# Key and value projections: values ahead of keys in three edge chunks, and all row terms added in one stretch

## The chip, the cores and the metric

The program runs on one core of a Trainium2 chip. The metric is the device time of one execution in microseconds (us), the median of several runs. Engines: PE (TensorE, matmuls), DVE (VectorE), ACT (ScalarE), POOL (GpSimd), SP (SyncE, which here only issues DMAs).

## The reference, cut to what matters

Two batches of 512 tokens with 1024 channels and a context of 1024 positions per batch go through four blocks. The change touches the first three, at their start:

```
x = x + tanh(g)*matmul(fake_quant(layernorm(x)), fake_quant(ctx))   # block 1
x = x + tanh(g)*(x1 @ W_org.T + sum_e coeff_e*(x1 @ down_e) @ up_e) # block 2, x1 = layernorm(x)
k = ctx @ Wk;  v = ctx @ Wv                                         # for block 3, attention
x = x + tanh(g)*(softmax(q k^T/sqrt(32)) v) @ Wo                    # block 3, q = layernorm(x) @ Wq
x = x + tanh(g)*moe(layernorm(x))                                   # block 4, two of three experts
```

With fake_quant(a) = (q - z)*s, the product in block 1 is a matmul of shifted integers plus a term for each row of x (`rterm`, from the row sums of the quantised x) and a term for each column of the context (`CB`, from its column sums).

## The kernel before, in words

Float32 matmuls are made of three bf16 ones: each operand is split into a high part and a low part (hi, lo), and hi*hi, hi*lo, lo*hi are summed in PSUM. Every engine has its own instruction list, written out by hand, and semaphores tie them together.

**Keys and values.** The context comes in 32 chunks of 128x1024 float32, in the order of the table `CHUNKS`: kind T (the transposed context, for keys and values) and kind N (the natural one, quantised for block 1). Chunks 0 to 7 are T of batch 0. Chunks 8 to 11 are T of batch 1, and its other four stand at 14, 16, 18 and 21 among N chunks. All from 22 on are N. SP loads them through a ring of 6 buffers, and waits in `load_context` until DVE is done with chunk n - 6 (`c_done`). For a T chunk, ACT writes the high part (L1076) and DVE the low part (L1345). For an N chunk, ACT scales (L1078), and DVE clips and rounds (L1390, L1392).

PE runs `kv_tile` (before, L643) once per T chunk. 12 matmuls of 512 columns (L666) add to the keys in banks 0 to 3, then 24 matmuls of 256 columns (L672) add to the values in banks 4 to 7. After the eighth chunk of a batch the banks are emptied in `kv_out`. ACT copies keys high (L1101) and half of the values (L1104), DVE copies the other half of the values (L1404) and takes keys low (L1409). Both wait for `kv_step`, that is for the whole of the eighth chunk. PE then begins the first chunk of batch 1 with keys, and waits for `k_lo` (DVE is done with the two banks).

**Block 1.** After the last T chunk PE sums columns (`column_sums`, L696, bank 4 + 2b and the next, so V must be out of them). It runs `quantised_tile(t)` for the 8 token tiles (L720, 16 matmuls each), whose operand SP turns by DMA (`turn_x`, L405) once all keys and values are through. The tiles write banks 0 to 3, so the keys must be out of them (`k_lo` 8). DVE makes the column term (`column_terms`, L1485). ACT adds the row term to each x tile (`add_rows`, L1108). POOL adds the column term behind it (`add_columns`, L548). DVE then adds the matmul result (`quantised_update`, L1502) and takes the layer norm of block 2 of it (L1358 and the small operations after it). ACT scales the tile (`scale_rows`, L1189), PE turns it (`turn_behind`, L708), ACT takes the high part (`turned_out`, L1195) and DVE the low part (`lo_parts`, L1492, in the middle of the next but one update).

ACT's list before, in the part the change touches:

```
chunks(26, 30); kv_out(1); chunks(30, 32)
for t in range(TB): add_rows(t)        # t = 0..3
scale_rows(0); scale_rows(1)
for t in range(2, TT):
    turned_out(t - 2); scale_rows(t)
    if t < 4: add_rows(2 * t); add_rows(2 * t + 1)
```

**Block 2.** PE goes through the LoRA queries (`lora_query`), eight hidden tiles (`lora_hidden`) and eight token tiles (`token_tile`), all L641. POOL splits the weights in two parts each (L516, L518), in the order down, lora_q, up, org, q, o, between its other work. Before the first token tile PE waits for all eight `org` weights (`wt_done`).

Of the kernel before, what the change touches and what calls it, by code (L numbers as in the profile page):

```python
# [32 lines left out]
KVD = KV_HEADS * HD  # L33
# [11 lines left out]
WT_AT = {name: sum(n for _, n in WT_LAYOUT[:i]) for i, (name, _) in enumerate(WT_LAYOUT)}  # L45
# [71 lines left out]
def build(nc, x, ctx_nat, ctx_t, wts, lora_q, lora_keys, scalars, gate_w, w1, b1, w2, b2, out):  # L117
    with ExitStack() as ctx:
# [3 lines left out]
        def sem(name):  # L122
            return ctx.enter_context(nc.semaphore(name))
# [6 lines left out]
        V = sb("V", [P, B * KT * KVD], F32)  # L130
# [57 lines left out]
        kb = [[R[1][:, b * half_r + i * 2 * SC:b * half_r + (i + 1) * 2 * SC] for i in range(2)] for b in range(B)]  # L188
# [27 lines left out]
        bank = [ctx.enter_context(nc.psum_tensor(f"bank{i}", [P, HALF], F32)) for i in range(8)]  # L216
# [16 lines left out]
        wt_done = sem("wt_done")  # L233
# [12 lines left out]
        xq_done = sem("xq_done")  # L246
        xq_t = [sem(f"xq_t{t}") for t in range(TT)]
        kv_step = sem("kv_step")
        rowq_done = sem("rowq_done")
        ln_bias = sem("ln_bias")  # L250
        k_hi = sem("k_hi")
        k_lo = sem("k_lo")
        v_act = sem("v_act")
# [380 lines left out]
        def _(pe):  # L634
# [8 lines left out]
                return mm  # L643


            def kv_tile(k, first, again, begin=False):
                def c(t, n0, n):
                    return t[:, k * D + n0:k * D + n0 + n]

                def w(t, n0, n):  # L650
                    return t[:, k * HALF + n0:k * HALF + n0 + n]

                for m in range(2):
                    if again:
                        pe.wait_ge(k_lo, 2 * (m + 1))
                    for a, r in ((kv_h, ct_h), (kv_h, ct_l), (kv_l, ct_h)):
                        if begin and m == 0:
                            if a is kv_l:
                                pe.wait_ge(kv_first, 2)
                            elif r is ct_l:  # L660
                                pe.wait_ge(c_done, 1)
                            else:
                                pe.wait_ge(kv_first, 1)
                                pe.wait_ge(c_act, 1)
                        for h in range(2):
                            mm = pe.matmul(bank[2 * m + h][:, :], w(a, m * P, P), c(r, h * HALF, HALF),  # L666
                                           start=first and a is kv_h and r is ct_h, stop=False, skip_group_check=True)
                for t in range(KT):
                    if again and t % 2 == 0:
                        pe.wait_ge((v_act, v_dve)[t // 4], t // 2 % 2 + 1)  # L670
                    for a, r in ((ct_h, kv_h), (ct_h, kv_l), (ct_l, kv_h)):
                        mm = pe.matmul(bank[4 + t // 2][:, (t % 2) * KVD:(t % 2 + 1) * KVD], c(a, t * P, P),  # L672
                                       w(r, KVD, KVD), start=first and t % 2 == 0 and a is ct_h and r is kv_h,
                                       stop=False, skip_group_check=True)
                return mm

            def keys_values(b):
                for k in range(KT):
                    begin = b == 0 and k == 0
                    if not begin:  # L680
                        if b == 0:
                            pe.wait_ge(wt_done, k // 2 + 1)
                        pe.wait_ge(c_done, CHUNKS.index(("T", b, k)) + 1)
                    mm = kv_tile(k, k == 0, b > 0 and k == 0, begin)
                    mm.then_inc(kv_step, 1)

            for _ in range(WARM):
                pe.matmul(bank[7][:, 0:P], identb[:, :], identb[:, :], start=True, stop=True)
# [112 lines left out]
            def token_tile(m, t, par, w_h, w_l, lora):  # L801

                pe.wait_ge(x_up, 2 * (m - 1))
                outs = [bank[2 * par][:, :], bank[2 * par + 1][:, :]]
                for k in range(KT):
                    cols = bass.ds(k * D + t * P, P)
                    mm = triple(outs, XTh[:, cols], XTl[:, cols],
                                [w_h[:, k * D + h * HALF:k * D + (h + 1) * HALF] for h in range(2)],
                                [w_l[:, k * D + h * HALF:k * D + (h + 1) * HALF] for h in range(2)],
                                k == 0, k == KT - 1 and not lora)  # L810
                if lora:
                    if isinstance(t, int) and t == 0:
                        pe.wait_ge(h_lo, B * JT)
                    for j in range(JT):
                        cols = bass.ds(j * D + t * P, P)
                        mm = triple(outs, HT_h[:, cols], HT_l[:, cols],
                                    [up_h[:, j * D + h * HALF:j * D + (h + 1) * HALF] for h in range(2)],
                                    [up_l[:, j * D + h * HALF:j * D + (h + 1) * HALF] for h in range(2)],
                                    False, j == JT - 1)
                mm.then_inc(nat_mm, 1)  # L820
# [28 lines left out]

            pe.wait_ge(cv_done, 4)  # L850
            pe.wait_ge(h_lo, JT + 1)
            pe.wait_ge(wt_done, WT_AT["q"])
            for t in range(TT):
                token_tile(TT + t, t, t % 2, org_h, org_l, True)
            first_queries()
# [207 lines left out]
        def _(act):  # L1063
# [30 lines left out]
                    act.wait_ge(rowq_done, t)  # L1094
                act.activation(junk_q, XQ[:, t * D:(t + 1) * D], ACT.Copy, accum_out=rowq[:, t:t + 1]).then_inc(rowq_done, 1)

            def kv_out(b):
                act.wait_ge(kv_step, KT * (b + 1))
                for i in (0, 1, 2, 3, 4, 5) if b == 0 else (4, 5, 0, 1, 2, 3):
                    if i < 4:  # L1100
                        act.activation(kb[b][0][:, i * HALF:(i + 1) * HALF], bank[i][:, :], ACT.Copy).then_inc(k_hi, 1)  # L1101
                    else:
                        at_v = b * KT * KVD + (i - 4) * HALF
                        act.activation(V[:, at_v:at_v + HALF], bank[i][:, :], ACT.Copy).then_inc(v_act, 1)  # L1104

            def add_rows(t):
                act.wait_ge(rterm_done, 1)
                act.activation(X[:, t * D:(t + 1) * D], X[:, t * D:(t + 1) * D], ACT.Identity,  # L1108
                               bias=rterm[:, t:t + 1]).then_inc(x_row, 1)

            def chunks(first, last):
                for n in range(first, last):
                    chunk(n)
# [20 lines left out]
            root(4, 0)  # L1134
            chunks(8, 9)
            scale_x(4)
            chunks(9, 11)
            kv_out(0)
            chunks(11, 12)
            row_sum(3)  # L1140
            root(5, 1)
            chunks(12, 15)
# [11 lines left out]
            chunks(23, 26)  # L1154
            row_sum(7)
            act.wait_ge(rowq_done, TT)
            chunks(26, 30)
            kv_out(1)
            chunks(30, 32)
            for t in range(TB):  # L1160
                add_rows(t)
            act.wait_ge(const_in, 48)

# [49 lines left out]
            for t in range(2, TT):  # L1213
                turned_out(t - 2)
                scale_rows(t)
                if t < 4:
                    add_rows(2 * t)
                    add_rows(2 * t + 1)
            lora_exp(0)
            turned_out(TT - 2)  # L1220
            hidden_out(0)
# [87 lines left out]
            for s in range(SLOTS):  # L1309
                b = s // TOPK  # L1310
# [24 lines left out]
        def _(dve):  # L1335
# [62 lines left out]
                dve.wait_ge(xq_sc, t + 1)  # L1398
                clip_round(xn[t % 2][:, :], XQ[:, t * D:(t + 1) * D], xq_clip, t, xq_done)

            def kv_out(b):
                def values(i):
                    at_v = b * KT * KVD + (2 + i) * HALF
                    dve.tensor_copy(V[:, at_v:at_v + HALF], bank[6 + i][:, :]).then_inc(v_dve, 1)  # L1404

                def keys_lo(i):
                    dve.wait_ge(k_hi, 4 * b + i + 1)
                    cols = slice(i * HALF, (i + 1) * HALF)
                    dve.tensor_tensor(kb[b][1][:, cols], bank[i][:, :], kb[b][0][:, cols], ALU.subtract).then_inc(k_lo, 1)  # L1409

                dve.wait_ge(kv_step, KT * (b + 1))
                values(0)
                if b == 0:
                    for i in range(4):
                        keys_lo(i)
                    values(1)
                else:
                    values(1)
                    for i in range(4):
                        keys_lo(i)  # L1420


            def constants():
                dve.wait_ge(sc_in, 16)
# [27 lines left out]
            def chunks(first, last):  # L1452
                for n in range(first, last):
                    chunk(n)
# [9 lines left out]
            x_step(3)  # L1464
            chunks(7, 8)
            x_step(4)
            chunks(8, 11)
            kv_out(0)
            x_step(5)
            chunks(11, 16)  # L1470
            x_step(6)
# [1 line left out]
            x_step(7)  # L1473
            chunks(20, 23)
            quantise_x(7)
            chunks(23, 29)
            kv_out(1)
            dve.wait_ge(rowq_done, TT)
            dve.tensor_scalar(rterm[:, :], rowq[:, :], qc[:, 5:6], qc[:, 4:5], ALU.add, ALU.mult).then_inc(rterm_done, 1)
            chunks(29, 32)  # L1480

            def column_terms(b):
                dve.wait_ge(cs_mm, b + 1)
# [392 lines left out]
```

## Time and profile before

| | us |
|---|---|
| median of 3 runs | 1254.35 (1251.49 to 1257.41) |
| the profiled execution | 1259.31 |
| its span in the profile | 1257.5 |
| PE busy in the span | 1222.9 (97%) |
| DVE busy | 821.9 (65%) |
| ACT busy | 476.4 (38%) |
| POOL busy | 681.7 (54%) |

The span is the time from the first to the last instruction, and the profiled execution lasts 1.8 us longer. Times in the rows are us from the span's start. A share of busy time is a mean over stages. The change lies between 44 and 205 us, so it is the rows of that part that tell.

### The profile page before, as it was taken

To read this page: it belongs to the slowest core of one execution; us is meant where nothing else is said; L and a number is where in the kernel's file an instruction comes from. 1 tells how busy PE (TensorE), PEld (TensorE's weight loads), DVE (VectorE), ACT (ScalarE), POOL (GpSimd) and SP (SyncE) were. 2 spreads that over 40 slices of the span, in tenths; PEclk is the share of its full clock that TensorE was granted. 3 is DMA by queue.
4 is the path that set the end of the run, shared out by engine and by line. 5 is a ranking of instruction groups with operands and counts; after the bars stand their busy time and mean duration, and the time that the engine had idled before them with its cause. 6 is when DMAs were issued, how large, how long until landed. Compare 5 with 4: busy or idle time off the path is not lost.

```text
span 1257.5 us, 16924 instructions
## 1 busy us (share of the span) xinstructions
PE 1222.9 (97%) x6504; PEld 512.1 (41%) x6504; DVE 821.9 (65%) x1417; ACT 476.4 (38%) x826; POOL 681.7 (54%) x300
## 2 busy tenths in 40 slices
PE   8998899999999899999999999999989999999998
PEld 6564444444444322222222222234434444444444
DVE  7997731433456778998999989335538855737622
ACT  4774521000100467777777677743242010010000
POOL 6005898500033478888989889870164553624510
PEclk9999999999999999999999999999989999999999
DMA  9566143311332145453545444443493443523301
GB/s 356 171 245 154 65 134 115 86 34 34 79 129 92 59 96 113 107 117 87 120 106 112 95 103 104 84 84 60 113 213 105 140 126 100 184 85 101 117 15 52
DMA packets 86764, 141.20 MB, mean 112 GB/s; under 512 B 49056, under 2 KB 59296, under 8 KB 82592
## 3 DMA queue, kind: packets, MB, share of 16 engines
q1 hardware_dynamic: 45840, 94.03, 23.7%
q0 software_dynamic: 4608, 33.56, 13.2%
q10 hardware_dynamic: 36240, 12.60, 5.2%
q8 instruction: 48, 0.79, 0.3%
q14 instruction: 28, 0.23, 0.1%
HBM read 85.49 MB, written 10.49 MB: 76 GB/s over the span
## 4 chain that ended last, share of the span: by engine, by line
PE 79%; DVE 12%; DMA 2%; POOL 2%; ACT 2%; issue 1%; ACTq 0%; SPq 0%; POOLq 0%; DVEq 0%
PE bank L641 46%; PE bank L879 9%; DVE mxp L1616 8%; PE bank L866 6%; PE bank L948 5%; PE bank L911 5%; PE bank L666 3%; PE bank L672 3%; DVE xn L1606 2%; DMA stage_c<-w_in 1%; DMA R<-R 1%; POOL R L607 1%; POOL R L629 1%; PE bank L720 1%; POOL X L548 1%
## 5 line engine op out<-in xcount | busy, mean ns | idle before, releaser
L1616 DVE TENSOR_REDUCE mxp<-bank 128x1 f32<-128x512 f32 x512 | 320.6, 680 | 60.6 <-PE bank L866 60.3
L1261 ACT ACTIVATE R<-bank 128x512 f32<-128x512 f32 x512 | 273.9, 602 | 116.7 <-PE bank L948 113.5
L641 PE MATMUL bank<-XTh,R 128*128 128x512 bf16 x896 | 279.3, 381 | 4.7 <-POOL R L629 4.5
L607 POOL TENSOR_TENSOR R<-R 128x2048 f32<-128x2048 f32 x48 | 218.6, 4555 | 35.4 <-ACT R L1261 29.4
L641 PE MATMUL bank<-R 128*128 128x512 bf16 x960 | 209.2, 379 | 0.0
L641 PE MATMUL bank<-XTl,R 128*128 128x512 bf16 x448 | 170.7, 381 | 0.0
L629 POOL TENSOR_TENSOR R<-stage_pair,R 128x1024 bf16<-128x1024 f32 x32 | 75.4, 2371 | 138.6 <-DVE R L1770 84.1
L641 PEld LDWEIGHTS bank<-R 128*128 128x128 bf16 x960 | 93.9, 98 | 113.3
L866 PE MATMUL bank<-R 96*128 96x512 bf16 x352 | 134.6, 382 | 4.6 <-DVE mxp L1616 3.0
L879 PE MATMUL bank<-R,stage_c 128*32 128x512 f32 x1024 | 137.1, 607 | 0.5 <-ACT R L1261 0.5
L948 PE MATMUL bank<-R 98*128 98x512 bf16 x352 | 134.4, 382 | 2.1 <-ACT R L1261 2.1
L641 PEld LDWEIGHTS bank<-XTh,R 128*128 128x128 bf16 x896 | 88.0, 98 | 112.1 <-POOL R L629 5.4
L516 POOL TENSOR_TENSOR R<-stage_pair,zero 128x1024 f32 (+1 forms) x35 | 67.2, 1920 | 77.4 <-DMA stage_pair<-wts_in 74.5
L629 POOL TENSOR_TENSOR R<-stage_c,R 128x1024 bf16<-128x1024 f32 x32 | 73.7, 2315 | 59.8 <-DVE R L1770 50.2
L1319 ACT ACTIVATE R<-bank,b1t 128x512 f32<-128x512 f32 x32 | 21.6, 686 | 198.1 <-PE bank L641 198.1
L866 PEld LDWEIGHTS bank<-R 96*128 96x128 bf16 x352 | 34.2, 97 | 112.2 <-DVE mxp L1616 84.7
L518 POOL TENSOR_TENSOR R<-stage_pair,R 128x1024 f32 (+1 forms) x35 | 75.9, 2167 | 5.3 <-POOL R L516 4.7
L1606 DVE RECIPROCAL xn<-p_total 128x128 f32<-128x128 f32 x64 | 59.2, 937 | 27.6 <-POOL xn L589 27.6
L607 POOL TENSOR_TENSOR stage_pair<-R 128x2048 f32<-128x2048 f32 x16 | 73.7, 4604 | 4.3 <-ACT R L1261 3.2
L911 PE MATMUL bank<-R,XTh 128*128 128x512 bf16 x256 | 69.7, 379 | 0.8 <-issue 0.8
L1815 DVE SCALAR_TENSOR_TENSOR X<-xn,TV,X 128x512 f32<-128x512 f32 x32 | 67.4, 2147 | 0.1
L1084 ACT ACTIVATE lnv<-lnv 128x1 f32<-128x1 f32 x32 | 6.5, 202 | 158.7 <-DVE lnv L1365 138.3
(194 smaller groups left out, 1502.0 us busy)
## 6 DMA issues: line engine op xcount, KB each, us to landing
stage_pair<-wts_in SPq DMA_DIRECT2D x35, 512.0 KB, 3.7
R<-R POOLq DMA_DIRECT2D x16, 1024.0 KB, 6.9
stage_pair<-R POOLq DMA_DIRECT2D x16, 1024.0 KB, 7.0
stage_pair<-w_in SPq DMA_DIRECT2D x32, 512.0 KB, 3.5
stage_c<-w_in SPq DMA_DIRECT2D x32, 512.0 KB, 3.6
R<-q_scr SPq DMA_DIRECT2D x48, 128.0 KB, 2.4
XTh<-ctx_t_in SPq DMA_DIRECT2D x11, 512.0 KB, 7.7
XTh<-ctx_nat_in SPq DMA_DIRECT2D x9, 512.0 KB, 3.9
```

What stands on the lines that cost most here:

```text
L518: pool.tensor_tensor(lo, stage_w[stage][:, :], hi, ALU.subtract).then_inc(wt_done, 1)
L607: pool.tensor_tensor(PS[(0, 1, 2, 1)[j]], PB[2 * j % 4], PB[2 * j % 4 + 1], ALU.add).then_inc(p_add, 1)
L629: pool.tensor_tensor(lo[:, cols], stage_e[(n - N_WT) % RING_E][:, :], hi[:, cols], ALU.subtract).then_inc(wt_done, 1)
L641: mm = pe.matmul(o, a, m, start=first and a is ah and bs is bh, stop=last and a is al)
L866: pe.matmul(bank[s_bank(u)][:, :], QS[g % 3][0:96, h * S + qt * P:h * S + (qt + 1) * P], KS[g % 3][0:96, kh * HALF:(kh + 1) * HALF], start ...
L879: mm = pe.matmul(out_bank[h * HD:(h + 1) * HD, :], weights, probs[:, h * S:(h + 1) * S], start=first, stop=last)
L911: mm = pe.matmul(outs[h], a[i][:, cols], b[i][:, k * D + h * HALF:k * D + (h + 1) * HALF], start=k == 0 and i == 0, stop=k == KT - 1 and i ...
L948: pe.matmul(bank[t_bank(g, t)][:, :], KS[g % 3][0:98, kt * P:(kt + 1) * P], QS[g % 3][0:98, h * S:(h + 1) * S], start=True, stop=True).the ...
L1261: act.activation(PB[kt % 4][:, h * S:(h + 1) * S], bank[t_bank(g, t)][:, :], ACT.Exp, scale=float(HD) ** -0.5).then_inc(exp_done, 1)
L1606: dve.reciprocal(rec[:, cols], p_sum[:, cols]).then_inc(rec_done, 1)
L1616: dve.tensor_reduce(mxp[head // REP % 2][:, m, n // 2, n % 2:n % 2 + 1], bank[s_bank(u)][:, :], AX.X, ALU.max).then_inc(s_max, 1)
L1815: dve.scalar_tensor_tensor(out=xh, in0=b2b[:, hc], scalar=TV[:, j * TT + t:j * TT + t + 1], in1=xh, op0=ALU.mult, op1=ALU.add).then_inc(eo ...
```

## The change

1. `kv_tile` is split into `keys_tile` and `values_tile`. In three edge chunks (the eighth of batch 0, the first and the eighth of batch 1) the values come ahead of the keys. The value tiles are taken in the order 0, 1, 4, 5, 2, 3, 6, 7.
2. A new semaphore `kv_vals` rises after the values of the eighth chunk. `kv_out` is split into `values_out`, which waits for `kv_vals`, and `keys_out`, which waits for `kv_step`, on ACT and on DVE.
3. The chunks of context are placed anew around them. Batch 0: ACT and DVE have only chunk 8 ahead of `values_out(0)`, chunk 9 between the two, chunk 10 behind. Batch 1: chunks up to 30 come ahead of `values_out(1)`, chunk 31 between, and none behind. The row term `rterm` is made ahead of `values_out(1)`.
4. ACT adds all eight row terms in one stretch behind `keys_out(1)`.
5. Token tile 0 of block 2 waits for each `org` weight apart, in place of all eight.

```diff
+            def keys_tile(b, k):
                 for m in range(2):
-                    if again:
+                    if b > 0 and k == 0:
                         pe.wait_ge(k_lo, 2 * (m + 1))
...
+            def values_tile(b, k):
+                for t in (0, 1, 4, 5, 2, 3, 6, 7):
+                    if b > 0 and k == 0 and t % 2 == 0:
                         pe.wait_ge((v_act, v_dve)[t // 4], t // 2 % 2 + 1)
...
-                    mm = kv_tile(k, k == 0, b > 0 and k == 0, begin)
-                    mm.then_inc(kv_step, 1)
+                    if k == KT - 1:
+                        values_tile(b, k).then_inc(kv_vals, 1)
+                        keys_tile(b, k).then_inc(kv_step, 1)
+                    elif b > 0 and k == 0:
+                        values_tile(b, k)
+                        keys_tile(b, k).then_inc(kv_step, 1)
+                    else:
+                        keys_tile(b, k)
+                        values_tile(b, k).then_inc(kv_step, 1)
...
                 for k in range(KT):
+                    if lora and t == 0:
+                        pe.wait_ge(wt_done, WT_AT["org"] + k + 1)
...
-            pe.wait_ge(wt_done, WT_AT["q"])
...
-            def kv_out(b):
+            def values_out(b):
+                act.wait_ge(kv_vals, b + 1)
...
+            def keys_out(b):
                 act.wait_ge(kv_step, KT * (b + 1))
...
-            chunks(9, 11)
-            kv_out(0)
-            chunks(11, 12)
+            values_out(0)
+            chunks(9, 10)
+            keys_out(0)
+            chunks(10, 12)
...
-            chunks(26, 30)
-            kv_out(1)
-            chunks(30, 32)
-            for t in range(TB):
+            chunks(26, 31)
+            values_out(1)
+            chunks(31, 32)
+            keys_out(1)
+            for t in range(TT):
                 add_rows(t)
...
                 scale_rows(t)
-                if t < 4:
-                    add_rows(2 * t)
-                    add_rows(2 * t + 1)
...
-            chunks(8, 11)
-            kv_out(0)
+            chunks(8, 9)
+            values_out(0)
+            chunks(9, 10)
+            keys_out(0)
+            chunks(10, 11)
...
-            chunks(23, 29)
-            kv_out(1)
+            chunks(23, 31)
             dve.wait_ge(rowq_done, TT)
             dve.tensor_scalar(rterm[:, :], rowq[:, :], qc[:, 5:6], qc[:, 4:5], ALU.add, ALU.mult).then_inc(rterm_done, 1)
-            chunks(29, 32)
+            values_out(1)
+            chunks(31, 32)
+            keys_out(1)
```

What this moves, on the two engines that PE waits for. First DVE's list at the end of keys and values, before (V from a bank is a values copy, R from a bank a keys low, rterm the row term, XTh or stage_c a chunk in its ring buffer, and the last row the column term):

```order
L1404 COPY V<-bank 128x512 x2
L1409 TENSOR_TENSOR R<-bank,R 128x512 x4
L1479 TENSOR_SCALAR rterm<-rowq,qc 128x8
L1390 TENSOR_SCALAR XTh<-XTh 128x1024
L1392 TENSOR_SCALAR R<-XTh 128x1024
L1390 TENSOR_SCALAR stage_c<-stage_c 128x1024
L1392 TENSOR_SCALAR R<-stage_c 128x1024
L1390 TENSOR_SCALAR stage_c<-stage_c 128x1024
L1392 TENSOR_SCALAR R<-stage_c 128x1024
L1485 TENSOR_SCALAR R<-bank,qc 128x512 x2
```

and in the changed kernel (where the lines have other numbers):

```order
L1404 TENSOR_SCALAR XTh<-XTh 128x1024
L1406 TENSOR_SCALAR R<-XTh 128x1024
L1404 TENSOR_SCALAR stage_c<-stage_c 128x1024
L1406 TENSOR_SCALAR R<-stage_c 128x1024
L1486 TENSOR_SCALAR rterm<-rowq,qc 128x8
L1419 COPY V<-bank 128x512 x2
L1404 TENSOR_SCALAR stage_c<-stage_c 128x1024
L1406 TENSOR_SCALAR R<-stage_c 128x1024
L1426 TENSOR_TENSOR R<-bank,R 128x512 x4
L1494 TENSOR_SCALAR R<-bank,qc 128x512 x2
```

Two of the three last chunks moved ahead of the values copies, the third stands between values and keys, and nothing is left between the keys and the column term.

ACT's list in block 1, before (V and R from a bank are the copies, X the row terms, lnv the root of a norm, xn the scaled rows, XTh from a bank the high parts of a turned tile):

```order
L1104 ACTIVATE V<-bank 128x512 x2
L1101 ACTIVATE R<-bank 128x512 x4
L1078 ACTIVATE stage_c<-stage_c,sc,rs 128x1024 x2
L1108 ACTIVATE X<-X,rterm 128x1024 x4
L1084 ACTIVATE lnv<-lnv 128x1
L1189 ACTIVATE xn<-X,lnv 128x1024
L1084 ACTIVATE lnv<-lnv 128x1
L1189 ACTIVATE xn<-X,lnv 128x1024
L1195 ACTIVATE XTh<-bank 128x4x128 x2
L1084 ACTIVATE lnv<-lnv 128x1
L1189 ACTIVATE xn<-X,lnv 128x1024
L1108 ACTIVATE X<-X,rterm 128x1024 x2
```

and in the changed kernel:

```order
L1114 ACTIVATE V<-bank 128x512 x2
L1091 ACTIVATE stage_c<-stage_c,sc,rs 128x1024
L1119 ACTIVATE R<-bank 128x512 x4
L1123 ACTIVATE X<-X,rterm 128x1024 x8
L1097 ACTIVATE lnv<-lnv 128x1
L1206 ACTIVATE xn<-X,lnv 128x1024
L1097 ACTIVATE lnv<-lnv 128x1
L1206 ACTIVATE xn<-X,lnv 128x1024
L1212 ACTIVATE XTh<-bank 128x4x128 x2
L1097 ACTIVATE lnv<-lnv 128x1
L1206 ACTIVATE xn<-X,lnv 128x1024
L1212 ACTIVATE XTh<-bank 128x4x128 x2
```

The two pairs of row terms that stood between the scaled rows and the high parts of tiles 1 and 2 are gone from there.

## Rows read from the trace of the kernel before

**Rows 1.** The page: the chain that ended last, by engine.

```profile
PE 79%; DVE 12%; DMA 2%; POOL 2%; ACT 2%; issue 1%; ACTq 0%; SPq 0%; POOLq 0%; DVEq 0%
```

**Rows 2.** The chain in order of time: start, us, what.

```profile
91.85 2.59 PE bank L666 x12
...
194.14 156.80 PE bank L641 x726
```

**Rows 3.** Timeline of PE, 51 to 146: start, us, engine, line, work [idle before <-releaser].

```profile
53.54 4.44 PE L666 MATMUL bank<-R 128*128 128x512 bf16 x12 [2.10 <-DVE R L1409]
...
98.49 3.61 PE L696 MATMUL bank<-R,onesb 128*128 128x512 bf16 x16 [1.43 <-DVE V L1404]
...
130.69 1.06 PE L708 MATMUL bank<-identf,xn 128*128 128x128 f32 x8 [3.10 <-DVE XTl L1492]
...
138.31 1.23 PE L708 MATMUL bank<-identf,xn 128*128 128x128 f32 x8 [3.10 <-DVE XTl L1492]
139.32 5.18 PE L720 MATMUL bank<-R 128*128 128x512 bf16 x16
...
145.22 0.38 PE L641 MATMUL bank<-XTh,stage_c 128*128 128x512 bf16 x1
```

**Rows 4.** Windows: us, busy PE, PEld, DVE, ACT, POOL, granted PE clock, DMA share, GB/s.

```profile
54.00:56.00 2.00, 2.00 (x6) 0.71 (x5) 2.00 (x5) 2.00 (x4) 0.00 (x0) 0.50 0.23 89
56.00:93.00 37.00, 37.00 (x254) 24.70 (x253) 35.75 (x70) 28.83 (x34) 0.00 (x0) 0.98 0.72 249
132.00:134.00 2.00, 2.00 (x11) 0.91 (x10) 1.86 (x7) 0.96 (x1) 0.50 (x1) 1.00 0.00 0
140.00:142.00 2.00, 2.00 (x6) 0.72 (x5) 1.89 (x6) 1.34 (x2) 1.92 (x3) 0.50 0.00 0
```

**Rows 5.** Timeline of DVE, 49 to 147.

```profile
49.03 2.36 DVE L1345 TENSOR_TENSOR R<-XTh,R 128x1024 bf16<-128x1024 f32 x2 [1.12 <-ACT R L1076]
...
52.10 2.48 DVE L1409 TENSOR_TENSOR R<-bank,R 128x512 bf16<-128x512 f32 x4
...
97.10 1.29 DVE L1404 COPY V<-bank 128x512 f32<-128x512 f32 x2 [3.70 <-PE bank L672]
...
101.30 0.69 DVE L1390 TENSOR_SCALAR XTh<-XTh 128x1024 f32<-128x1024 f32 x1
...
105.29 1.40 DVE L1485 TENSOR_SCALAR R<-bank,qc 128x512 f32<-128x512 f32 x2
109.20 1.41 DVE L1502 SCALAR_TENSOR_TENSOR X<-bank,qc,X 128x512 f32<-128x512 f32 x2 [2.51 <-POOL X L548]
...
125.30 1.40 DVE L1502 SCALAR_TENSOR_TENSOR X<-bank,qc,X 128x512 f32<-128x512 f32 x2
...
129.25 1.29 DVE L1492 TENSOR_TENSOR XTl<-bank,XTh 128x512 bf16<-128x512 f32 x2 [1.82 <-ACT XTh L1195]
...
140.54 1.40 DVE L1502 SCALAR_TENSOR_TENSOR X<-bank,qc,X 128x512 f32<-128x512 f32 x2
...
146.24 1.40 DVE L1502 SCALAR_TENSOR_TENSOR X<-bank,qc,X 128x512 f32<-128x512 f32 x2
```

**Rows 6.** Timeline of ACT, the row terms.

```profile
102.24 4.29 ACT L1108 ACTIVATE X<-X,rterm 128x1024 f32<-128x1024 f32 x4
...
126.57 2.17 ACT L1108 ACTIVATE X<-X,rterm 128x1024 f32<-128x1024 f32 x2
```

**Rows 7.** Timeline of POOL, 106 to 205.

```profile
106.83 9.28 POOL L548 TENSOR_TENSOR X<-X,R 128x1024 f32<-128x1024 f32 x4 [78.45 <-DVE R L1485]
...
127.84 4.66 POOL L548 TENSOR_TENSOR X<-X,R 128x1024 f32<-128x1024 f32 x2 [3.62 <-ACT X L1108]
...
140.00 1.90 POOL L558 TENSOR_TENSOR stage_c<-stage_c,zero 128x1024 bf16<-128x1024 f32 x1
...
204.96 1.89 POOL L516 TENSOR_TENSOR R<-stage_pair,zero 128x1024 f32 x1 [2.79 <-PE bank L641]
```

**Rows 8.** Timeline of SP's queue: the turning of the quantised x.

```profile
97.09 11.01 SPq L405 DMA_TRANSPOSE R<-XTl x8
```

More of the change, by code:

```diff
@@ L248, in build @@
         kv_step = sem("kv_step")
+        kv_vals = sem("kv_vals")
         rowq_done = sem("rowq_done")
@@ L643, in triple, with chunk_part, weight_part @@
                 return mm
[L646 to L651, printed above, removed]
+            def chunk_part(t, k, n0, n):
+                return t[:, k * D + n0:k * D + n0 + n]
+            def weight_part(t, k, n0, n):
+                return t[:, k * HALF + n0:k * HALF + n0 + n]
+            def keys_tile(b, k):
                 for m in range(2):
-                    if again:
+                    if b > 0 and k == 0:
                         pe.wait_ge(k_lo, 2 * (m + 1))
                     for a, r in ((kv_h, ct_h), (kv_h, ct_l), (kv_l, ct_h)):
-                        if begin and m == 0:
+                        if b == 0 and k == 0 and m == 0:
                             if a is kv_l:
@@ L665, in kv_tile @@
                         for h in range(2):
[L666 to L669, printed above, removed]
+                            mm = pe.matmul(bank[2 * m + h][:, :], weight_part(a, k, m * P, P), chunk_part(r, k, h * HALF, HALF),
+                                           start=k == 0 and a is kv_h and r is ct_h, stop=False, skip_group_check=True)
+                return mm
+            def values_tile(b, k):
+                for t in (0, 1, 4, 5, 2, 3, 6, 7):
+                    if b > 0 and k == 0 and t % 2 == 0:
                         pe.wait_ge((v_act, v_dve)[t // 4], t // 2 % 2 + 1)
                     for a, r in ((ct_h, kv_h), (ct_h, kv_l), (ct_l, kv_h)):
-                        mm = pe.matmul(bank[4 + t // 2][:, (t % 2) * KVD:(t % 2 + 1) * KVD], c(a, t * P, P),
-                                       w(r, KVD, KVD), start=first and t % 2 == 0 and a is ct_h and r is kv_h,
+                        mm = pe.matmul(bank[4 + t // 2][:, (t % 2) * KVD:(t % 2 + 1) * KVD], chunk_part(a, k, t * P, P),
+                                       weight_part(r, k, KVD, KVD), start=k == 0 and t % 2 == 0 and a is ct_h and r is kv_h,
                                        stop=False, skip_group_check=True)
@@ L678, in keys_values @@
                 for k in range(KT):
-                    begin = b == 0 and k == 0
-                    if not begin:
+                    if b > 0 or k > 0:
                         if b == 0:
@@ L1095, in row_sum @@
                 act.activation(junk_q, XQ[:, t * D:(t + 1) * D], ACT.Copy, accum_out=rowq[:, t:t + 1]).then_inc(rowq_done, 1)
-            def kv_out(b):
-                act.wait_ge(kv_step, KT * (b + 1))
[L1099 to L1104, printed above, removed]
+            def values_out(b):
+                act.wait_ge(kv_vals, b + 1)
+                for i in range(2):
+                    at_v = b * KT * KVD + i * HALF
+                    act.activation(V[:, at_v:at_v + HALF], bank[4 + i][:, :], ACT.Copy).then_inc(v_act, 1)
+            def keys_out(b):
+                act.wait_ge(kv_step, KT * (b + 1))
+                for i in range(4):
+                    act.activation(kb[b][0][:, i * HALF:(i + 1) * HALF], bank[i][:, :], ACT.Copy).then_inc(k_hi, 1)
             def add_rows(t):
@@ L1399, in quantise_x, with values_out, keys_out @@
                 clip_round(xn[t % 2][:, :], XQ[:, t * D:(t + 1) * D], xq_clip, t, xq_done)
-            def kv_out(b):
-                def values(i):
+            def values_out(b):
+                dve.wait_ge(kv_vals, b + 1)
+                for i in range(2):
                     at_v = b * KT * KVD + (2 + i) * HALF
                     dve.tensor_copy(V[:, at_v:at_v + HALF], bank[6 + i][:, :]).then_inc(v_dve, 1)
-                def keys_lo(i):
+            def keys_out(b):
+                dve.wait_ge(kv_step, KT * (b + 1))
+                for i in range(4):
                     dve.wait_ge(k_hi, 4 * b + i + 1)
@@ L1409, in keys_lo @@
                     dve.tensor_tensor(kb[b][1][:, cols], bank[i][:, :], kb[b][0][:, cols], ALU.subtract).then_inc(k_lo, 1)
[L1411 to L1420, printed above, removed]
             def constants():
```

## The prediction

> **What bounds the kernel now.** I read the chain of waits first. PE holds 79% of it and DVE 12% [rows 1], so only a place where PE waits, or where PE's waits are set by another engine, can give time. Then I read PE's timeline over the part that the change touches, to find these places. There are three.
>
> At the boundary of the batches PE stands still for 2.10 us until DVE has taken keys low. The 12 matmuls behind it take 4.44 us [rows 3], where the same 12 take 2.59 elsewhere, 0.216 each [rows 2]. The granted clock is 0.50 there, the lower of PE's two levels (1.2 GHz in place of 2.4), in the window 54 to 56 [rows 4]. Together 2.10 + 1.85 = 3.95 us.
>
> At the end of keys and values PE waits 1.43 us for DVE's copies of V [rows 3].
>
> In block 1, PE waits for the low part of each turned tile, up to 3.10 us a time [rows 3]. What sets the pace is the chain of updates on DVE. Three updates start at 125.30, 140.54 (two later) and 146.24 [rows 5]. The two periods up to 140.54 are 7.62 us each, the one behind it is 5.70. The long ones hold a 1.82 us wait for ACT, which had put a pair of row terms (2.17 us) ahead of the high part [rows 5, 6]. From 145.22 on PE has its own work as its bound: one piece of the chain, from 194.14, is 156.8 us of matmuls without a break [rows 2]. So a start of that stretch that is earlier by n us makes everything behind it earlier by n.
>
> DVE is the second bound. From 56 to 93 it is busy 35.75 of 37 us [rows 4]. It then idles 3.70 us ahead of its V copies, since PE is not done [rows 5].
>
> **The change, part by part.**
>
> *Boundary of the batches.* Values of the eighth chunk come first, so both engines empty banks 4 to 7 while PE makes keys (2.59 us). The next chunk begins with values (2.62 us), and in that time the keys leave banks 0 to 3. DVE took its first two keys-low operations until about 2 us after PE's end, and all four until 3.15 us (52.10 + 2.48 against 53.54 - 2.10) [rows 5]; the keys banks are wanted 2.62 and 3.9 us after it. PE's wait and the slow stretch behind it go: PE ended keys and values at 97.06 (98.49 - 1.43), and would end them at 93.1. What is late next is DVE. It does the same work in another order, but must wait for ACT between: before, the last keys-low is followed by one V copy (0.6 us), now by the low part of chunk 10 (1.18, half of 2.36) [rows 5]. So `x_step(5)` starts some 0.6 later, and as DVE has no slack until 93, it ends chunk 28 at 93.40 (97.10 - 3.70) + 0.6 = 94.0. This first gain is therefore worth nothing yet: PE stands before DVE.
>
> *End of keys and values.* DVE now has two more chunks ahead of its V copies. One chunk costs 1.33 us ((105.29 - 101.30)/3 [rows 5]). 94.0 + 2.66 + 0.2 for the row term = 96.85, V copies 1.25, done at 98.1. PE's column sums start at 98.2, against 98.49. PE idles 5.1 us there, not 1.43. Then come chunk 31 (to 99.4), keys low 2.4 (to 101.8) and the column term at 101.85, which started at 105.29 before [rows 5]: 3.45 us earlier. It also needs the column sums, 3.45 us of PE (16 x 0.216): 98.2 + 3.45 = 101.65. Tile 0 needs the keys out, 101.8, as before. ACT has the copies and the scaling of chunk 31 beside it, and its eight row terms (4.29/4 = 1.07 each [rows 6]) run from about 98 to 106.5, each ahead of its column term. The first root that ACT owes DVE comes after that.
>
> *PE's clock.* The idle 5.1 us is the new cost. The rows have four gaps on PE, of 2.10, 1.43, 3.10 and 3.10 us. After the first and the last the clock fell (0.50), after the others it did not (1.00 at 132 to 134, behind the first 3.10; 16 matmuls in 3.61 us behind the 1.43) [rows 3, 4]. A fall cost 1.85 us over 12 matmuls, and 1.57 over the 16 matmuls at 139.32 (5.18 against 3.61) [rows 3]. Bounds: 0 (no fall), and 16 + 16 matmuls of column sums and tile 0 all at the lower level, 32 x 0.216 = 6.9. I take 1.7, the mean of the two rows, since the gap is longer than any of the four. The column sums then end at 103.35, the column term starts at 103.4, and 3.45 shrinks to 1.9 us. POOL's first addition follows it (1.54 us behind its start, 106.83), and the first update starts 2.37 us later still [rows 5, 7]: 107.3 against 109.20. Tile 0 ends at 106.8, in time. The Trainium skill, page "TensorE: Matmul & The Clock Gate", section "HAM oscillation — how this bites in real kernels", tells that PE idle between bursts of matmuls can put its clock back to the half rate, so that each next burst begins slow. By that rule alone the fall at 98 is certain; by the count of rows it is two of four.
>
> *Row terms in one stretch.* With none between scaled rows and high part, the two periods of 7.62 become 5.70 like the next one: 2 x 1.92 = 3.84 us. They are not on ACT's path any more, where before they were late for POOL as well (3.62 us idle on POOL) [rows 7]. PE must keep up: its work from tile 0 to `turn_behind(2)` puts the turned tiles at most 1 us behind DVE's chain, with gaps of about 1.4 in place of 3.10. So the second fall of the clock goes too. It was worth 0.4 us: 145.22 lay 4.68 behind the update at 140.54, and would lie 4.3 behind it (2.05 to the low part, 1.27 for it, 0.1, and 0.88 for eight transposes).
>
> *The weights behind it.* POOL works from 140.00 to 202.17 (204.96 - 2.79), 62.2 us, all of it weight splits, and PE needs its last `org` part at about 204.7 [rows 7]. If POOL stayed and PE moved, this would bind. But POOL's first four additions start 1.9 earlier, and the other four find their rows ready: 104.9 + 9.3, + 8.1 for two weight splits (116.11 to 124.22), + 9.3 = 131.6 in place of 140.00. That is 8.4 earlier, more than PE moves. `lora_q` takes two more operations, some 4 us, and PE wants it at 139. The waits per weight at token tile 0 have nothing to hide: cost 0, and if POOL were late they would soften it.
>
> *Queues.* SP issues the eight turning DMAs (11.01 us from 97.09 [rows 8]) once PE is through, so 4 us earlier. Tile 0 is not waiting for the first, as it starts no earlier. SP's keys out and weights behind them come as early. The ring loads of chunks 29 to 31 follow DVE, 0.6 later, and have the time of the chunks before to land.
>
> **Sum**, against the profiled execution: 1.9 + 3.84 + 0.4 = 6.15 us, so 1259.31 - 6.15 = 1253.2. That execution is 5 us above the median. One difference can be in this very place: the 1.85 us after the boundary gap need not be there in each execution, as gaps without a fall show. Where they are missing, the kernel before is faster by 1.85 (PE ends sooner, DVE has 3.70 to spare) and the changed one is not. The gain is then 4.3. I take the middle, 5.25, off the median of the runs: **1249.1 us**.
>
> **The rivals.**
>
> *A, the forecast:* DVE bounds the end of keys and values, one fall of the clock behind the long gap. 4.3 to 6.15 us, 1248.2 to 1250.05. Chance 0.47.
>
> *B, the clock holds or costs little:* the column term really is 3.45 earlier. 3.45 + 3.84 + 0.4 = 7.7, less up to 1.85 as above: 1246.7 to 1248.5. For it: a gap of 3.10 without a fall. Against it: the gap is 5.1. Chance 0.20.
>
> *C, the gain of the row terms is swallowed:* PE or POOL becomes the bound of block 1, for instance because `lora_q` or the turned tiles are late, and only the first term is left: 1.9 us, 1252.5; with neither, 1254.35. For it: PE is slack by some 1 us only. Against it: POOL's 8.4 us. Chance 0.22.
>
> *D, slower:* the clock, once down at 98, stays at the lower level through column sums and tiles 0 to 3, 96 matmuls x 0.216 = 20.7 us, as the tiles are then PE's bound. Less the 7.7: +13, 1267. It is slower from 7.7 us of such loss on (36 matmuls). For it: there are small gaps between these tiles that could hold it down. Against it: both falls in the rows were over within 12 to 16 matmuls. Chance 0.04.
>
> The remaining 0.07 is for what I do not see, either side.
>
> **How the numbers follow.** A measurement of this kernel can tell about 0.5%, 6.3 us, from no change; faster by that is below 1248.1. Of A a quarter lies there with the scatter of the runs (5.9 us between highest and lowest of three), 0.12; of B four fifths, 0.16; of C none; the remainder 0.04, and the scatter of the median itself lifts the total to 0.38. Slower: D and a share of the remainder, 0.05. Within: 0.57. The range goes from B with scatter below, 1244.5, to C without either term, 1253.
>
> **What would show it.** PE has no wait at the boundary, and its clock stays at 1.00 there. PE ends keys and values near 93.1 and the column sums start near 98.2, with 0.50 granted behind them. DVE has no idle time ahead of its V copies. The column term starts near 103.4. All updates from the second on are 5.7 us apart, and the first LoRA query is at about 139. Wrong would be: a gap at 93 much shorter than 5 us; the gap between updates above 6; a wait of PE for POOL in block 2.

## The result, and the profile after

| | before | changed |
|---|---|---|
| median of 20 runs, us | 1256.83 (1251.49 to 1263.28) | 1253.85 (1249.73 to 1256.35) |
| ratio of the times | | 0.9972, 95% interval 0.9963 to 0.9981 |
| the profiled execution, us | 1259.31 | 1254.74 |
| its span, us | 1257.5 | 1252.9 |
| first LoRA query on PE, us from the start | 145.22 | 139.30 |

The change makes the kernel faster by 0.28%, which is 3.5 us (2.4 to 4.7 by the interval, so clear of zero). The forecast was 1249.1 us in a range from 1244.5 to 1253, and the measured median lies above it.

In the profiled pair nearly each step came where the prediction had put it. PE's timeline of the changed kernel, the part that answers to [rows 3]:

```profile
53.64 5.34 PE L668 MATMUL bank<-R 128*128 128x512 bf16 x24
...
90.11 2.75 PE L668 MATMUL bank<-R 128*128 128x512 bf16 x12
97.90 5.50 PE L708 MATMUL bank<-R,onesb 128*128 128x512 bf16 x16 [5.03 <-DVE V L1419]
103.24 7.07 PE L732 MATMUL bank<-R 128*128 128x512 bf16 x32
...
132.70 1.06 PE L720 MATMUL bank<-identf,xn 128*128 128x128 f32 x8 [1.18 <-DVE XTl L1501]
133.60 3.62 PE L732 MATMUL bank<-R 128*128 128x512 bf16 x16
138.40 1.06 PE L720 MATMUL bank<-identf,xn 128*128 128x128 f32 x8 [1.18 <-DVE XTl L1501]
139.30 0.38 PE L642 MATMUL bank<-XTh,stage_c 128*128 128x512 bf16 x1
```

The boundary of the batches has no wait any more: keys of two chunks follow each other, 24 matmuls in 5.34 us. PE ends keys and values at 92.87, and idles 5.03 us. The column sums behind that gap take 5.50 us, against 3.61 before. The gaps in block 1 are 1.18 us in place of 3.10.

The windows of the changed kernel (columns as in [rows 4]) give the clock:

```profile
54.00:56.00 2.00, 2.00 (x11) 0.88 (x9) 2.00 (x4) 2.00 (x4) 0.00 (x0) 1.00 0.78 306
56.00:92.80 36.80, 36.80 (x254) 24.60 (x252) 35.59 (x70) 28.55 (x34) 0.00 (x0) 1.00 0.73 240
93.00:97.90 4.90, 0.00 (x1) 0.03 (x2) 4.80 (x10) 4.82 (x8) 0.00 (x0) 0.70 1.03 209
98.00:100.00 2.00, 2.00 (x6) 0.61 (x6) 1.97 (x4) 2.00 (x3) 0.00 (x0) 0.50 0.97 187
102.00:104.00 2.00, 2.00 (x11) 0.92 (x10) 0.49 (x1) 2.00 (x3) 0.00 (x0) 1.00 0.95 183
```

At the boundary it stays at 1.00. It falls in the idle time (0.70 is the mean of it), is at 0.50 when the column sums begin, and is back at 1.00 from 102 on.

DVE's timeline of the changed kernel, which answers to [rows 5]:

```profile
96.52 1.28 DVE L1419 COPY V<-bank 128x512 f32<-128x512 f32 x2
97.71 0.68 DVE L1404 TENSOR_SCALAR stage_c<-stage_c 128x1024 f32<-128x1024 f32 x1
98.43 0.69 DVE L1406 TENSOR_SCALAR R<-stage_c 128x1024 bf16<-128x1024 f32 x1
99.04 2.48 DVE L1426 TENSOR_TENSOR R<-bank,R 128x512 bf16<-128x512 f32 x4
103.51 1.41 DVE L1494 TENSOR_SCALAR R<-bank,qc 128x512 f32<-128x512 f32 x2 [1.99 <-PE bank L708]
107.45 1.41 DVE L1511 SCALAR_TENSOR_TENSOR X<-bank,qc,X 128x512 f32<-128x512 f32 x2 [2.53 <-POOL X L549]
...
123.54 1.40 DVE L1511 SCALAR_TENSOR_TENSOR X<-bank,qc,X 128x512 f32<-128x512 f32 x2
...
134.94 1.40 DVE L1511 SCALAR_TENSOR_TENSOR X<-bank,qc,X 128x512 f32<-128x512 f32 x2
```

DVE has no idle time ahead of its V copies, since it now comes to them after PE is through. The column term starts at 103.51 (forecast 103.4) and had to wait 1.99 us for the slow column sums. The first update starts at 107.45 (forecast 107.3, before 109.20). Two periods lead from 123.54 to 134.94, 5.70 each.

POOL (answers to [rows 7]) has its four last additions in one piece, and its wait for PE ahead of the `q` weights is longer, so no weight holds PE:

```profile
122.45 9.29 POOL L549 TENSOR_TENSOR X<-X,R 128x1024 f32<-128x1024 f32 x4
131.70 1.89 POOL L559 TENSOR_TENSOR stage_c<-stage_c,zero 128x1024 bf16<-128x1024 f32 x1
...
199.05 1.89 POOL L517 TENSOR_TENSOR R<-stage_pair,zero 128x1024 f32 x1 [5.35 <-PE bank L642]
```

So the profiled pair has 5.92 us at the LoRA query and still 5.91 at 199 us (204.96 - 199.05), where 6.15 was forecast. At the end of the span 4.6 us are left (1257.5 - 1252.9). Yet the runs gave 3.5. Two questions remained: which part of the change gives the time, and why the runs show less than the profiles.

### The profile page after: what moved, and what is told of

It reads as the page before. It is cut to its first block, busy times and chain, and to the rows that moved or that the text cites. A ratio compares the mean times of both kernels' runs of the same rounds, so it can differ in the third digit from the quotient of the medians.

```text
span 1252.9 us, 16926 instructions
## 1 busy us (share of the span) xinstructions
PE 1223.0 (98%) x6504; PEld 511.6 (41%) x6504; DVE 822.5 (66%) x1417; ACT 476.8 (38%) x826; POOL 681.5 (54%) x300
## 4 chain that ended last, share of the span: by engine, by line
PE 76%; DVE 16%; DMA 2%; issue 2%; POOL 2%; ACT 1%; ACTq 0%; SPq 0%; POOLq 0%; DVEq 0%
PE bank L642 46%; PE bank L892 9%; DVE mxp L1625 8%; PE bank L879 6%; PE bank L961 5%; PE bank L924 5%; DVE xn L1615 2%; PE bank L678 2%; PE bank L668 1%; DVE R L1406 1%; DMA stage_c<-w_in 1%; DVE R L1359 1%; DMA R<-R 1%; POOL R L608 1%; POOL R L630 1%
## 5 line engine op out<-in xcount | busy, mean ns | idle before, releaser
L1805 DVE CAST R<-R 128x512 bf16<-128x512 f32 x32 | 17.5, 547 | 75.1 <-ACT R L1333 75.1
```

## The experiments

All were timed beside the kernel before, in two batches on one chip each. The medians of before were 1256.94 us (29 runs) and 1257.13 us (23 runs). The gains below are the ratio's. The plain differences of the medians are up to 1.1 us away from them (6.1 in place of 7.2 for the widest), and lie within the intervals. The rival theories: the two terms of the sum are both real; or only one of them is, and the other comes from a slow stretch in the profiled execution of before that other executions don't have.

### The row terms alone

```diff
-            for t in range(TB):
+            for t in range(TT):
                 add_rows(t)
...
                 scale_rows(t)
-                if t < 4:
-                    add_rows(2 * t)
-                    add_rows(2 * t + 1)
```

> The kernel before, with nothing but the eight row terms in one stretch behind the last chunks. Theory (both terms of the sum are real and add up): update periods on DVE fall from 7.62 to 5.70 us twice, the first update stays at about 109.2 (107.3 if the clock did not fall at the batch boundary), the first LoRA query comes at about 141; 3.8 to 4.3 us faster than before in the mean. Rival (the row terms have slack elsewhere and the gain of the change is only in DVE's order): no more than 1 us.

Measured: 1253.32 us, ratio 0.9974 (0.9961 to 0.9987), which is 3.3 us. DVE's timeline of this kernel:

```profile
109.23 1.41 DVE L1499 SCALAR_TENSOR_TENSOR X<-bank,qc,X 128x512 f32<-128x512 f32 x2 [2.54 <-POOL X L548]
...
125.33 1.40 DVE L1499 SCALAR_TENSOR_TENSOR X<-bank,qc,X 128x512 f32<-128x512 f32 x2
131.03 1.40 DVE L1499 SCALAR_TENSOR_TENSOR X<-bank,qc,X 128x512 f32<-128x512 f32 x2
136.73 1.40 DVE L1499 SCALAR_TENSOR_TENSOR X<-bank,qc,X 128x512 f32<-128x512 f32 x2
```

The first update stands where it was, the two periods are 5.70, and the LoRA query is at 141.09, 4.13 us earlier. This term is real, in the trace and in the runs (1.6 to 4.9 us by the interval), and this edit alone brings as much as the whole change, as far as the intervals can tell.

### The split alone

```diff
             keys_out(1)
-            for t in range(TT):
+            for t in range(TB):
                 add_rows(t)
...
                 scale_rows(t)
+                if t < 4:
+                    add_rows(2 * t)
+                    add_rows(2 * t + 1)
```

> The changed kernel, with the row terms back in their old places (four, then two and two). Theory: the first update at about 107.4, the two long periods of 7.62 us are back, so the LoRA query comes at about 143.5; against before 1.9 us faster where before has its slow stretch at the batch boundary, and about 0 where it has not, so 0 to 1.9 in the mean. Rival (the split carries the gain): 3 us or more.

Measured: 1257.19 us, ratio 1.0002 (0.9991 to 1.0013): no gain that shows, and at most 1.1 us by the interval. In its profile the LoRA query is at 143.50, 1.72 us ahead of the profile of before. So this term of the sum is in the pair of profiles and does not show in the runs. DVE's column term waits 2.41 us for the column sums here, which take 5.92 us behind a gap of 5.04: the same fall of the clock, a second time.

### The kernel before, a second profile

> The kernel before, once more, for a second profile. Theory (the slow stretch behind the boundary of the batches is not there in every execution, which is why the split alone gained 1.7 us in the profile and nothing in the runs): in some profile the 12 matmuls behind the boundary gap take less than 4.2 us and the keys and values end before 96.5. Rival: they take 4.2 to 4.4 again, as in both profiles so far that have this gap, and the keys and values end at 97.06.

Measured: 1257.78 us, ratio 1.0004 (0.9988 to 1.002). PE's timeline, DVE's, and the window that has 0.50 in [rows 4]:

```profile
53.69 2.54 PE L666 MATMUL bank<-R 128*128 128x512 bf16 x11 [2.59 <-DVE R L1409]
...
96.96 3.40 PE L696 MATMUL bank<-R,onesb 128*128 128x512 bf16 x15 [1.64 <-DVE V L1404]
```

```profile
95.36 1.29 DVE L1404 COPY V<-bank 128x512 f32<-128x512 f32 x2 [2.02 <-PE bank L672]
...
103.55 1.40 DVE L1485 TENSOR_SCALAR R<-bank,qc 128x512 f32<-128x512 f32 x2
107.47 1.41 DVE L1502 SCALAR_TENSOR_TENSOR X<-bank,qc,X 128x512 f32<-128x512 f32 x2 [2.52 <-POOL X L548]
...
131.18 1.40 DVE L1502 SCALAR_TENSOR_TENSOR X<-bank,qc,X 128x512 f32<-128x512 f32 x2
```

```profile
54.00:56.00 2.00, 2.00 (x11) 0.89 (x10) 2.00 (x5) 2.00 (x4) 0.00 (x0) 1.00 0.31 112
```

The gap at the boundary is there, and the clock does not fall behind it. (The row has 11 of the 12 matmuls, so the record of one is missing. The next group starts at 56.07 and 12 matmuls at 0.216 us take 2.59, so they began at 53.48, and PE waited 2.4 us and not the 2.59 of the row.) Keys and values end at 95.32, 1.74 us sooner than in the first profile. The column term starts at 103.55 and the first update at 107.47. In the changed kernel these are 103.51 and 107.45. Without the fall at the boundary, then, the split gains nothing at this place. The LoRA query is at 143.17, and the changed kernel's 139.30 is 3.87 us ahead of it, which is the row terms' 3.84. Three profiles have this gap now (before, the row terms alone, this one), two with a fall and one without.

How often it falls in the runs was not counted. If two of three is the rule, the split should still gain 1.2 us in the mean (two thirds of 1.74), just outside the interval of the split alone, and three profiles are few. A rival is not excluded: the split gains something at the boundary and loses it to falls elsewhere. The mean granted clock over its 12 runs is 0.9912, against 0.9940 for the 29 of before. The fall behind its long gap is in that number, and whether others are was not looked into.

### PE kept busy in its idle time

```diff
+            pe.wait_ge(v_act, 4)
+            for _ in range(23):
+                pe.matmul(bank[4][:, :], identb[:, :], kv_h[:, 0:HALF], start=True, stop=True)
             pe.wait_ge(v_dve, 4)
-            pe.wait_ge(v_act, 4)
             column_sums(0)
...
-            chunks(26, 31)
+            chunks(26, 30)
             values_out(1)
-            chunks(31, 32)
+            chunks(30, 32)
```

(The second piece is ACT's list.)

> The changed kernel, with 23 matmuls of 512 columns on PE in its idle time behind the last keys (they write bank 4, whose values ACT has already copied; ACT copies values one chunk sooner for that). Theory (the fall of the clock behind the long gap delays the column sums and with them everything): column sums of 16 matmuls in 3.5 us in place of 5.4, column term at about 101.5, 1.7 to 2.0 us faster than the changed kernel, so 5.2 to 5.5 faster than before. Rival (the fall is not on the path, or another wait is just behind it): as the changed kernel, about 3.5.

Measured: 1250.8 us, ratio 0.9943 (0.9927 to 0.9958), which is 7.2 us. PE's timeline, and a window:

```profile
93.21 5.12 PE L768 MATMUL bank<-R,identb 128*128 128x512 bf16 x23 [0.24 <-ACT V L1116]
98.17 3.62 PE L708 MATMUL bank<-R,onesb 128*128 128x512 bf16 x16
```

```profile
98.00:100.00 2.00, 2.00 (x11) 0.93 (x10) 1.97 (x4) 2.00 (x3) 0.00 (x0) 1.00 0.97 183
```

The clock holds, 16 column sums take 3.62 us, the column term starts at 101.90 and the LoRA query is at 137.70, 1.6 us ahead of the changed kernel. So the fall was on the path and cost 1.6 us, close to the 1.7 taken. Its cause is shown too: PE's idle time, since work that computes nothing removes it. ACT's earlier copy of the values is no rival for this, as the column sums start 0.27 us later than in the changed kernel (98.17 against 97.90). All six runs have a mean clock of 0.996 or 0.997, where the changed kernel's twenty have 0.991 to 0.996.

### Values and keys out first, one chunk, then the column term

```diff
-            chunks(23, 31)
+            chunks(23, 29)
+            values_out(1)
+            keys_out(1)
             dve.wait_ge(rowq_done, TT)
...
-            values_out(1)
-            chunks(31, 32)
-            keys_out(1)
...
+            chunks(29, 30)
             dve.wait_ge(k_out, 32)
             column_terms(0)
+            chunks(30, 32)
```

(DVE's list. ACT's has `values_out(1)`, `keys_out(1)` ahead of chunks 30 and 31.)

> The changed kernel, with DVE and ACT emptying values and keys ahead of the last three chunks, and DVE making the first column term behind the first of these three. Theory (DVE's order decides, and PE's idle time there is only a shadow of it): PE waits about 2.2 us, not 5, behind the last keys, the column term starts at about 100.2, the first update at 103 to 104, and the LoRA query about 3.5 to 4.4 us earlier than in the changed kernel; 7 to 8 us faster than before. Rival (PE is by then the bound of block 1, so that only the clock's share is saved): 2 us better than the changed kernel, 5.5 faster than before.

Measured: 1255.68 us, ratio 0.9983 (0.9969 to 0.9998), which is 2.1 us. Both theories missed. By the runs it cannot be told from the changed kernel (0.9972, 0.9963 to 0.9981), but in its profile the LoRA query is at 140.88, 1.6 us later than there. DVE's timeline and POOL's:

```profile
98.83 1.41 DVE L1493 TENSOR_SCALAR R<-bank,qc 128x512 f32<-128x512 f32 x2
100.15 0.68 DVE L1404 TENSOR_SCALAR stage_c<-stage_c 128x1024 f32<-128x1024 f32 x1
100.87 2.73 DVE L1406 TENSOR_SCALAR R<-stage_c 128x1024 bf16<-128x1024 f32 x1
103.52 2.85 DVE L1404 TENSOR_SCALAR stage_c<-stage_c 128x1024 f32<-128x1024 f32 x1
106.40 2.71 DVE L1406 TENSOR_SCALAR R<-stage_c 128x1024 bf16<-128x1024 f32 x1
109.03 1.40 DVE L1510 SCALAR_TENSOR_TENSOR X<-bank,qc,X 128x512 f32<-128x512 f32 x2
```

```profile
100.37 10.96 POOL L549 TENSOR_TENSOR X<-X,R 128x1024 f32<-128x1024 f32 x4 [71.59 <-DVE R L1493]
```

The column term is 4.7 us early, as wished. It also lets POOL begin at 100.37, and from then on DVE's clips and roundings take 2.7 to 2.85 us each in place of 0.69. POOL's four additions take 10.96 in place of 9.30. The first update comes at 109.03 and all that was gained is gone. The Trainium skill, page "SBUF — State Buffer", section "Who interferes with whom", states that DVE's `tensor_scalar` in its two-port mode and any GpSimd operation hold the same pair of ports for a whole instruction, so that one blocks the other fully. The trace agrees: each of the three lasts 2.0 to 2.2 us longer than alone, near one addition of POOL (9.30/4 = 2.33), and the next two experiments test it.

### The same, with POOL held back

```diff
+            pool.wait_ge(c_done, len(CHUNKS))
             add_columns(0)
```

> early_terms with one more wait: POOL begins its additions only when DVE is done with all 32 chunks. Theory (POOL beside DVE is what slows the clips): DVE's last two chunks take 2.66 us together, not 8.2, POOL starts at about 102.9 in place of 100.4, and still the first update comes at about 105.3, 3.7 us sooner than in early_terms; 5 to 6 us faster than before. Rival (POOL has no part in it): clips of 2.7 us and the first update at 109 or later.

Measured: 1250.73 us, ratio 0.9955 (0.9941 to 0.997), which is 5.7 us. DVE's timeline and POOL's:

```profile
99.87 0.68 DVE L1405 TENSOR_SCALAR stage_c<-stage_c 128x1024 f32<-128x1024 f32 x1
100.59 0.69 DVE L1407 TENSOR_SCALAR R<-stage_c 128x1024 bf16<-128x1024 f32 x1
101.20 0.69 DVE L1405 TENSOR_SCALAR stage_c<-stage_c 128x1024 f32<-128x1024 f32 x1
101.92 0.69 DVE L1407 TENSOR_SCALAR R<-stage_c 128x1024 bf16<-128x1024 f32 x1
105.14 1.41 DVE L1511 SCALAR_TENSOR_TENSOR X<-bank,qc,X 128x512 f32<-128x512 f32 x2 [2.53 <-POOL X L549]
```

```profile
102.75 9.31 POOL L549 TENSOR_TENSOR X<-X,R 128x1024 f32<-128x1024 f32 x4 [74.28 <-ACT X L1124]
```

POOL begins 2.4 us later, and the first update comes 3.9 us sooner. The wait on POOL is the only difference to the kernel before it, so POOL beside DVE was the cause.

### The column term behind all chunks

```diff
-            chunks(29, 30)
+            chunks(29, 32)
             dve.wait_ge(k_out, 32)
             column_terms(0)
-            chunks(30, 32)
```

(Against the kernel two experiments above, without POOL's wait.)

> As early_terms, but with the first column term behind all of the last three chunks, as it stands in the changed kernel, so that POOL adds nothing while DVE clips and rounds. Theory (in early_terms DVE's clip and round took 2.7 us in place of 0.7 because POOL was adding beside them): every clip and round takes 0.69 us, the column term starts at about 101.5 and the first update at about 105.4, against 109.03 in early_terms and 107.45 in the changed kernel; LoRA query at about 137.3; 5 to 6 us faster than before. Rival (the slow clips have another cause, the position behind the keys for instance): clips of 2.7 us again and no gain on the changed kernel.

Measured: 1251.09 us, ratio 0.9957 (0.9942 to 0.9972), which is 5.4 us. Column term at 101.26, first update at 105.20, LoRA query at 137.06, 2.2 us ahead of the changed kernel. PE's timeline:

```profile
94.87 5.30 PE L708 MATMUL bank<-R,onesb 128*128 128x512 bf16 x16 [2.18 <-DVE V L1419]
100.00 7.07 PE L732 MATMUL bank<-R 128*128 128x512 bf16 x31
```

The clock fell here too, behind a gap of only 2.18 us, and this time it cost nothing: the column sums end at 100.2, ahead of the column term's turn on DVE.

### The same, with PE kept busy

The kernel is the one just above. Ten matmuls stand where the 23 stood in "PE kept busy in its idle time", and ACT copies the values one chunk sooner.

> early_keys with 10 matmuls of 512 columns in the 2.2 us that PE still waits behind the last keys (as in warm). Theory (a fall of the clock there is off the path once PE is ahead of DVE, as the column sums have about 3 us of slack): as early_keys within 1 us in time, with a higher mean clock. Rival (each fall of the clock costs time wherever it is, since PE has little slack in block 1): 1.5 us or more faster than early_keys.

Measured: 1250.87 us, ratio 0.9957 (0.9942 to 0.9973): the same as without them. Its mean granted clock over the runs is no higher either (0.9945 against 0.9950), so that part of the expectation did not come. In its profile PE has no gap there (the ten matmuls from 93.06, the column sums at 95.36) and the LoRA query is at 137.59, no earlier than 137.06. Once DVE and not PE ends last, a fall at that place is free, as expected. By the runs, this kernel, the two above it and the 23 matmuls (5.4 to 7.2 us) cannot be told from each other.

## Why the prediction was wrong

**The level.** This step failed first. The forecast was set against the median of three runs, 1254.35 us. The median of 20 runs is 1256.83. These 2.5 us put the result outside the range: from 1254.35 the measured ratio would have led to 1250.8, well inside. The profiled execution (1259.31) was the other hint. I read its 5 us as its own slowness, and it was half that.

**The range.** Its upper end, "C without either term, 1253", does not fit rival C, which gives 1254.35 "with neither" and has a chance of 0.22. The measured 1253.85 lies between the two.

**The sum of the trace was right, in part by luck.** 6.15 us forecast, 5.92 measured at the LoRA query of the profiled pair. The first update came 1.75 earlier (forecast 1.9), the row terms gave 3.85 (3.84), and 0.32 came behind them (0.4). DVE bounded the end of keys and values, the column sums fell to the lower clock behind the long gap, and POOL's weights did not bind. Gaps in block 1 are 1.18 us, forecast 1.4. The luck is that the first and the last term stand on two falls of the clock, and the profile of before had both. Its second profile has neither, and the changed kernel is 3.87 ahead of it, less than the 4.3 that the prediction gave for that case.

**The term that was mis-sized** is the first: "I take the middle, 5.25". That counts half of the 1.9 us of the split, 0.95, though the prediction said itself that they stand on a fall of the clock at the batch boundary that need not be in each execution. The split alone measured 1.0002, and the second profile of before has the column term at 103.55 against 103.51. The right value is near zero at this place, so the row terms' 3.84 remain. The measured 3.5 us (2.4 to 4.7) agree with the row terms alone, 3.3 us (1.6 to 4.9). The runs are not sharp enough to say how the 1.7 us between 5.25 and 3.5 are shared: 0.95 for the split still lies within the interval of the split alone, and 3.84 + 0.4 within that of the row terms.

**Where the rest goes.** The profiles' 5.91 us at 199 us had become 4.6 at the end. They go in block 4, behind 938 us. ACT's row at 943.84 in the profile of before is at 937.56 in that of the changed kernel, 6.28 ahead. The one at 953.83 is at 949.25, 4.58 ahead. The same work between them, before and changed (us, busy PE, granted PE clock, DMA share, GB/s):

```profile
944.30:947.70 3.40, 3.40 (x17) 1.00 0.74 263
938.10:941.40 3.30, 3.30 (x9) 0.50 0.83 277
```

In 3.3 us PE gets through half as many matmuls, and that is the 1.7 us. Both profiles have another stretch at the lower clock just ahead of this one (0.57 in 933.5 to 940 before, 0.50 in 928 to 934.5 changed). This change does not touch that part, and the kernel before has such differences from one execution to the next: its second profile is 2.4 us ahead of the first at 850 us and 1.2 at the end, with a granted clock of 0.97 in 875 to 925 where the first has 1.00.

Over the runs the mean granted clock tells the same: among the 29 runs of before in the first batch, the ten at 0.993 have a mean of 1258.5 us and the three at 0.996 of 1254.0. So falls of the clock that differ between executions are worth as much as the change. The changed kernel's 20 runs, taken in another batch, have 0.9932 in the mean, before's 29 have 0.9940. Both profiles with the long gap have a fall behind it. Whether that explains all of the lower mean was not tested.

**The rivals.** B (the clock holds) falls: the fall came in both profiles with a gap of 5 us. C (the row terms are swallowed) falls: they are the gain. D (slower through a lasting lower clock) falls: the clock was back within the 16 column sums. That the split gains nothing where the boundary has no fall was named as a part of A, and not given the weight it needed.

**The waits per weight** at token tile 0 were not tried alone. POOL is done with `org` at 193.7 (199.05 - 5.35) in the changed kernel and PE comes 5 us later, so they had nothing to hide.

## What to carry to other kernels

Before a gain is booked for a wait that goes away, ask whether its cost was the wait or a fall of the clock behind it, and take a second profile: a fall may be in one execution and not in the next. Set the forecast against a level from enough runs: here the median of three lay 2.5 us from that of twenty, which is most of the gain measured. The work moved off the path of an engine chain (here two row terms out of ACT's turn in a 7.62 us period) was the gain that held in the trace and in the runs. Where DVE is the bound and PE idles for some us in its shadow, let DVE empty PE's banks first or give PE matmuls that compute nothing; each helped here. Check that no earlier release lets POOL run beside DVE's clips and roundings.

## What the runs showed of the hardware

- The same gap on PE can end with or without a fall of the granted clock. At the batch boundary 2.10 and 2.54 us were followed by 0.50, and about 2.4 us was not. A gap of 2.18 us fell in one kernel (16 matmuls in 5.30 us) and not in two others (3.61 us each). Both gaps of 5 us fell.
- 23 matmuls whose results are thrown away, 5.12 us of PE, made the kernel faster by 3.6 us against the changed one by the ratios (0.9943 against 0.9972). Each ratio is known to 1 or 2 us only, so the 1.6 us seen at the LoRA query may be all of it. The two profiles end 5.1 us apart (1252.9 - 1247.8), but there too later falls differ: the granted clock is 0.93 in 425 to 450 and 0.80 in 925 to 950 in the changed kernel, 1.00 and 0.93 with the 23 matmuls.
- DVE's clip or round of 128x1024 float32 takes 0.69 us alone and 2.7 to 2.85 us while POOL adds tiles of the same size, whereas DVE's updates, which read PSUM, keep their 1.40 us beside POOL (the update at 109.03 beside the additions that last until 111.3).
